# The middle bf16 part of a projection made on GpSimd, and the slots of transposes, expert and post steps placed anew

## The chip, the cores and the metric

The kernel runs on one core of a Trainium2 chip. The metric is the device time of one launch in microseconds. An engine's name in the rows: PE is TensorE, DVE VectorE, ACT ScalarE, POOL GpSimd, SP SyncE.

## The reference

Eight sequences of 512 tokens, 128 features, in fp32. Differential attention with 16 heads of size 8, then a layer norm, then a mixture of 8 experts of which each token uses 2, then a layer norm again. Cut to what is computed:

```python
q, k1, k2, v = (split_heads(x @ W.T) for W in (Wq, Wk1, Wk2, Wv))
a = softmax(causal(q @ k1.T * SCALE)) - sigmoid(lambda_logit) * softmax(causal(q @ k2.T * SCALE))
a = a / maximum(sum(abs(a), -1), 1e-6)
x = layernorm(x + merge_heads(a @ v) @ Wo.T)
xn = layernorm(x) * gamma + beta
w, idx = top_k(softmax(xn @ router_w.T / 1.5), 2)
h = silu(einsum('btd,edf->betf', xn, W1))
y = einsum('betf,efd->betd', h, W2)
out = layernorm(sum over e of wdense[e] * y[e] + x)
```

## The kernel before

**Slots.** All five engines run the same program of bodies; a body has 40 slots (SLOTS), one for each chunk of a batch's attention. A chunk is up to 512 score columns of one head pair: eight pairs times five kinds of chunk, which differ in how many query tiles they hold. Body b does the attention of batch b, prepares batch b+1 (the "prep" steps), and carries the "post" steps of the batches before: slot 48 of a post step means slot 8, one body later. Body -1 is the prologue; bodies 8 to 10 are the tail, in which only post steps are left. Each engine goes through its slots in order; between engines there are only semaphores. So a number in a table of slots sets the place of a step in each engine's queue, and nothing else.

**A chunk's way.** In slot c TensorE makes the scores of chunk c, twice (k = 0 and 1 for the two key sets), and VectorE takes their maxima (neg_max). In slot c+1 (LAG_EXP) ScalarE makes the exponentials into a ring of 7 (EXP_RING). VectorE makes the reciprocals of the sums (inv_l2). In slot c+4 (LAG_DIFF) GpSimd scales the second exponential and subtracts the first (a one-input operation at L623, a two-input one at L627); for one kind in five VectorE does it (L977). In slot c+4 as well (LAG_TRANS) TensorE transposes the difference into the one bank `trans`. In slot c+5 ScalarE copies it out (LAG_COPY), and VectorE sums its absolute values (LAG_ABS). From slot c+6 on TensorE multiplies with the values (LAG_PV). TensorE's transposes come last in a slot, ahead of the next slot's scores:

```python
for n, c in chunks(b, stages, slot, LAG_TRANS):
    pe.wait_ge(*diff_ready(n, c))
    pe.wait_ge(diffT_copied.sem, diffT_copied.after(m, used + 1))
```

**A projection step** ("proj", three of them: q, k1, k2) splits its fp32 result into three bf16 parts. TensorE multiplies in the step's slot, ScalarE makes part 0 (L716) in the same slot. One slot later VectorE makes `rest`, the result less part 0 (L854), and part 1, its cast (L858). Two slots later GpSimd makes part 2, `rest` less part 1 (L634). `rest` is one buffer: VectorE waits for part 2 of the step before. SyncE stores the parts PARTS_SLOT slots after the step, and loads the stack for the next batch's scores from slot STACK_SLOT on.

**Post steps.** "spread", "den_T", "divide" and "out_proj" end the attention: the division (L872) makes attnT on VectorE a slot after its number, TensorE's output projection (L1054) waits for it. "scatter" steps are indirect DMAs that GpSimd issues two slots after their number (L643); each sends 128 rows to their place in the list sorted by expert. "gather" steps bring the results back (L652). "hidden" and "expert" steps are the two matmuls of one of 15 tiles of sorted rows, with ScalarE's tanh between them and VectorE's hT (L933).

Of the kernel before, what the change touches and what calls it, by code (L numbers as in the profile page):

```python
# [52 lines left out]

LAG_EXP = 1
LAG_DIFF = 4
LAG_TRANS = 4
LAG_COPY = LAG_TRANS + 1
LAG_ABS = 5
LAG_DEN = LAG_ABS + 1
# [16 lines left out]


PV_ORDER = (1, 3, 2, 0)
V_SLOT = 7
PV_STEPS = ((7, 0, ((1, 0), (1, 1))), (8, 0, ((3, 0), (3, 1))), (9, 0, ((3, 2), (3, 3), (2, 0))),  # L80
            (9, 1, ((2, 1), (2, 2))), (9, 2, ((0, 0),)))


SIDE = {}
POST_SLOTS = {"spread": 8, "den_T": 10, "divide": 11, "out_proj": 12, "norms": 17, "xn_T": 21, "logits": 23, "router_exp": 24, "count": 29, "place": 31, "sorted": 43, "norm3": 96, "finish": 98}
HIDDEN_SLOTS = (45, 47, 49, 51, 53, 55, 59, 60, 64, 66, 68, 70, 72, 74, 76)
EXPERT_SLOTS = (48, 50, 52, 54, 56, 58, 62, 63, 67, 69, 71, 73, 75, 76, 78)
WEIGHT_SLOTS = (41, 43, 45, 47, 49, 51, 55, 56, 61, 62, 62, 66, 68, 69, 69)
TURN_SLOTS = (44, 51, 58, 66)
Y_OUT_SLOTS = (57, 67, 77, 83)  # L90
SCATTER_SLOTS = (31, 32, 33, 34, 35, 36, 37, 38)
GATHER_SLOTS = (82, 83, 85, 85, 86, 88, 89, 90)
COMBINE_SLOTS = (86, 86, 88, 90, 90, 91, 92, 93)
STACK_SLOT = 31
WEIGHTS_AHEAD = 4
PARTS_SLOT = 4
PREP_SLOTS = (15, 18, 23, 24, 25)


def units_of(c):  # L100
# [74 lines left out]
PARTS_STORED = (3, len(STORED), len(STORED))  # L175
# [19 lines left out]
def build(nc, x, wqT, wk1T, wk2T, wvT, woT, lam, gamma, beta, rwT, w12, out):  # L195
    ctx = ExitStack()
    with ctx:
# [37 lines left out]
        parts = sb("parts", [P, 3, 3, T], BF16)  # L235
        rest = sb("rest", [P, T])
# [79 lines left out]
        rest_made = signal("rest_made", 3)  # L316
        mid_made = signal("mid_made", 3)
        lo_made = signal("lo_made", 3)
        parts_out = signal("parts_out", sum(PARTS_STORED), 16)
# [46 lines left out]
        router_exp = signal("router_exp", 1)  # L366
# [202 lines left out]
        def _(pool):  # L569
# [29 lines left out]
            def body(b, stages):  # L599
                for slot in range(SLOTS):  # L600
                    for n, c in chunks(b, stages, slot, LAG_DIFF):
                        pair, kind = divmod(c, KINDS)
                        ring = ring_e(n, c)
                        count = pair * len(SUM_SETS) + SUM_SET_OF[kind] + 1
# [24 lines left out]
                    for task, n, bank in side_tasks(b, slot, 2 * LAG_SIDE):  # L629
                        name = task[1]  # L630
                        if name == "proj":
                            z = task[2]
                            pool.wait_ge(mid_made.sem, mid_made.after(n, z + 1))
                            nc.gpsimd.tensor_tensor(parts[:, z, 2, :], rest[:, :], parts[:, z, 1, :],  # L634
                                                    ALU.subtract).then_inc(lo_made.sem, 1)
# [128 lines left out]
        def _(dve):  # L764
# [69 lines left out]
            def body(b, stages):  # L834
                for slot in range(SLOTS):
# [10 lines left out]
                    for task, n, bank in side_tasks(b, slot, LAG_SIDE):  # L846
                        name = task[1]
                        if name == "proj":

                            z = task[2]  # L850
                            dve.wait_ge(psum_of(task).sem, psum_of(task).after(n, psum_count[task]))
                            dve.wait_ge(hi_made.sem, hi_made.after(n, z + 1))
                            dve.wait_ge(lo_made.sem, lo_made.after(n, z))
                            nc.vector.scalar_tensor_tensor(out=rest[:, :], in0=bank[:, :],  # L854
                                                           scalar=SCALE if z == 0 else 1.0, in1=parts[:, z, 0, :],
                                                           op0=ALU.mult, op1=ALU.subtract).then_inc(rest_made.sem, 1)
                            dve.wait_ge(rest_made.sem, rest_made.after(n, z + 1))
                            nc.vector.tensor_copy(parts[:, z, 1, :], rest[:, :]).then_inc(mid_made.sem, 1)  # L858
                        if name == "spread":

                            dve.wait_ge(den_done.sem, den_done.after(n, 4))
# [27 lines left out]
                        if name == "logits":  # L889
                            dve.wait_ge(psum_of(task).sem, psum_of(task).after(n, psum_count[task]))  # L890
                            logits = bank[:, 0:NT * E].rearrange("p (t e) -> p t e", t=NT)
# [72 lines left out]
                    for n, c in chunks(b, stages, slot, LAG_EXP + 2):  # L964
                        pair, kind = divmod(c, KINDS)
                        if kind in DVE_KINDS:
# [3 lines left out]
                            count = pair * len(DVE_KINDS) + DVE_KINDS.index(kind) + 1  # L970
# [209 lines left out]
```

## Time and profile before

| what | us |
|---|---|
| device time, median of 3 runs | 1151.64 |
| lowest and highest | 1149.92, 1158.81 |
| the profiled execution | 1164.99 |
| its span | 1163.2 |

The profiled execution took 13.35 us more than the median. Its first 46 us are the prologue, with the constants, the weights and the first projections. Seven batches then follow each other at up to 129 us a batch, and from about 1026 us on only post steps are left. The page gives busy shares; what an engine waits for stands in the view of waits and, in brackets behind an instruction, in the timeline ("[1.59 <-POOL exps L627]": idle for 1.59 us until GpSimd's L627 was done).

### The profile page before, as it was taken

The numbers are of one execution on the slowest core, as the hardware profiler recorded it, in microseconds if no ns is written. First come the engines' busy times: TensorE is split into PE (matmuls) and PEld (weight loads), VectorE is DVE, ScalarE is ACT, GpSimd is POOL, SyncE is SP. The second block draws the span as 40 slices with busy tenths as digits, with TensorE's granted clock in tenths as the row PEclk, the third lists the DMA queues.
The fourth block names the chain that finished last, engine by engine and source line by source line (L and its number), as shares of the span: only waits on it lengthen the run. The fifth ranks groups of instructions, "written<-read, shape, count | busy, mean of one in ns | idle before, by whom it ended". The sixth has DMA issues, their size and how long they took to land.

```text
span 1163.2 us, 27864 instructions
## 1 busy us (share of the span) xinstructions
PE 917.6 (79%) x8522; PEld 730.0 (63%) x8522; DVE 948.4 (82%) x2449; ACT 842.8 (72%) x2706; POOL 838.7 (72%) x1120
## 2 busy tenths in 40 slices
PE   2478867868888888978898979978897888968572
PEld 1255645647677676757676767757675777758561
DVE  1499999879998999979998999889998999725132
ACT  1499978679888788887878878887878878723130
POOL 3388977697768987798768977798769976851503
PEclk9588888679999799988998899988998999878696
DMA  3603400533246524662347415652347322245462
GB/s 102 176 2 95 107 1 16 138 93 124 77 143 167 164 71 128 176 188 72 104 135 181 145 57 154 157 179 92 114 130 193 116 73 83 79 142 189 162 208 62
DMA packets 117045, 139.38 MB, mean 120 GB/s; under 512 B 11042, under 2 KB 99490, under 8 KB 116898
## 3 DMA queue, kind: packets, MB, share of 16 engines
q1 hardware_dynamic: 112802, 129.21, 38.0%
q0 software_dynamic: 4096, 8.40, 2.5%
q8 instruction: 69, 1.13, 0.4%
q14 instruction: 78, 0.64, 0.2%
HBM read 107.81 MB, written 29.75 MB: 118 GB/s over the span
## 4 chain that ended last, share of the span: by engine, by line
DVE 31%; PE 18%; POOL 16%; issue 15%; ACT 12%; DMA 5%; SPq 2%; DVEq 1%; another core or an unknown queue 0%; POOLq 0%; ACTq 0%
DVE neg_max L988 13%; ACT exps L697 7%; DVE abs_sum L998 5%; POOL exps L627 5%; POOL exps L623 5%; POOL x_sorted_dram L643 4%; PE trans L1150 3%; ACT diffT L704 3%; PE side L1093 2%; PE scores L1116 2%; DVE hT L933 2%; DMA w_sb<-w_dram 2%; PE side L1099 2%; PE scores L1093 1%; DVE acc L945 1%
## 5 line engine op out<-in xcount | busy, mean ns | idle before, releaser
L697 ACT ACTIVATE exps<-scores,neg_max 128x512 f32<-128x512 f32 (+3 forms) x1024 | 542.0, 548 | 113.0 <-DVE neg_max L988 106.9
L988 DVE TENSOR_REDUCE neg_max<-scores 128x1 f32<-128x512 f32 (+3 forms) x896 | 423.5, 524 | 58.0 <-PE scores L1118 53.5
L627 POOL TENSOR_TENSOR exps<-exps 128x512 f32<-128x512 f32 x256 | 326.1, 1274 | 21.4
L623 POOL TENSOR_SCALAR exps<-exps,inv_l,lam_l 128x384 f32<-128x384 f32 (+3 forms) x448 | 273.6, 618 | 91.5 <-DVE inv_l L963 79.2
L1150 PE MATMUL trans<-ident,exps 128*128 128x128 f32 x1280 | 236.4, 314 | 117.6 <-ACT diffT L704 61.9
L1116 PE MATMUL scores<-stack 72*128 72x512 bf16 (+3 forms) x1024 | 275.3, 337 | 16.3 <-DMA stack<-parts_dram 15.8
L1150 PEld LDWEIGHTS trans<-ident,exps 128*128 128x128 f32 x1280 | 158.9, 158 | 179.6 <-issue 99.3
L697 ACT ACTIVATION_READ_ACCUMULATOR exps<-scores,neg_max 128x1 f32 x1024 | 232.6, 227 | 0.0
L704 ACT ACTIVATE diffT<-trans 128x512 f32<-128x512 f32 x320 | 195.7, 612 | 45.7 <-PE trans L1150 44.4
L998 DVE TENSOR_REDUCE abs_sum<-exps 128x1 f32<-128x512 f32 (+3 forms) x448 | 222.6, 519 | 5.6 <-POOL exps L627 5.6
L1118 PE MATMUL scores<-causal_bf,ident_bf 128*128 128x128 bf16 x1024 | 211.0, 239 | 0.0
L1116 PEld LDWEIGHTS scores<-stack 72*128 72x128 bf16 x1024 | 111.5, 109 | 69.1 <-DMA stack<-parts_dram 16.0
L1093 PE MATMUL side<-xgT,w_sb 128*128 128x128 f32 x792 | 123.9, 305 | 3.6 <-DMA w_sb<-w_dram 1.7
L1099 PE MATMUL side<-w_sb,hT 128*128 128x128 f32 x824 | 116.4, 285 | 6.8 <-DVE hT L933 5.6
L1093 PEld LDWEIGHTS side<-xgT,w_sb 128*128 128x128 f32 x792 | 109.3, 213 | 11.2 <-issue 3.3
L1118 PEld LDWEIGHTS scores<-causal_bf,ident_bf 128*128 128x128 bf16 x1024 | 111.8, 109 | 7.0
L1099 PEld LDWEIGHTS side<-w_sb,hT 128*128 128x128 f32 x824 | 103.4, 197 | 14.3 <-DVE hT L933 5.8
L1139 PE MATMUL heads<-diffT,v_sb 128*32 128x128 f32 x2560 | 108.1, 287 | 2.8 <-issue 2.8
L652 POOL DMA_INDIRECT y_back<-y_sorted_dram,place_int x64 | 65.6, 1026 | 47.1 <-issue 45.7
L643 POOL DMA_INDIRECT x_sorted_dram<-xh,place_int x64 | 68.4, 1069 | 40.5 <-DVE owner_int L924 30.6
L1139 PEld LDWEIGHTS heads<-diffT,v_sb 128*32 128x32 f32 x2560 | 62.8, 112 | 37.7 <-issue 22.5
L750 ACT ACTIVATE tanh_sb<-side 128x512 f32<-128x512 f32 x99 | 60.3, 609 | 32.3 <-PE side L1093 29.6
(138 smaller groups left out, 916.5 us busy)
## 6 DMA issues: line engine op xcount, KB each, us to landing
w_sb<-w_dram SPq DMA_DIRECT2D x120, 512.0 KB
stack<-parts_dram SPq DMA_DIRECT2D x288, 96.0 KB
parts_dram<-parts SPq DMA_DIRECT2D x104, 128.0 KB, 2.4
xg<-x_sorted_dram SPq DMA_DIRECT2D x24, 256.0 KB
y_sorted_dram<-y_sorted SPq DMA_DIRECT2D x24, 256.0 KB, 4.3
x_in<-x_dram SPq DMA_DIRECT2D x8, 256.0 KB, 4.4
x_res<-x_dram SPq DMA_DIRECT2D x8, 256.0 KB, 4.6
o_dram<-y_out SPq DMA_DIRECT2D x8, 256.0 KB, 2.3
```

Of the source, the lines that this page charges most:

```text
L623: nc.gpsimd.tensor_scalar(diff[:, ring, col:col + w], exps[:, ring, 1, col:col + w], inv_l2[:, i:i + 1], lam_l1[:, i:i + 1], ALU.mult, ALU ...
L627: nc.gpsimd.tensor_tensor(diff[:, ring, :], diff[:, ring, :], exps[:, ring, 0, :], ALU.subtract)\
L697: nc.scalar.activation(exps[:, ring, k, col:col + w], scores[:, c % 2, k, col:col + w], ACT.Exp, bias=neg_max[:, c % 2, k, i:i + 1], accum ...
L704: nc.scalar.activation(diffT[:, ring_d(n, c), :], trans[:, :], ACT.Copy)\
L988: nc.vector.tensor_reduce(neg_max[:, c % 2, k, i:i + many], scores[:, c % 2, k, col:col + many * w].rearrange("p (i w) -> p i w", w=w), AX ...
L998: nc.vector.tensor_reduce(abs_sum[:, place:place + (many - 1) * step + 1:step], diff[:, ring_e(n, c), col:col + many * w].rearrange("p (i ...
L1093: last = nc.tensor.matmul(bank[:, f * P:(f + 1) * P], w12_sb[:, w, f * P:(f + 1) * P], xgT[:, j // NT % 2, j % NT, :], start=True, stop=True)
L1099: last = nc.tensor.matmul(bank[:, 0:D], hT[:, (n * TILES + j) % 2, f, :], w12_sb[:, (n * TILES + j) % WEIGHTS_AHEAD, F + f * D:F + (f + 1) ...
L1116: nc.tensor.matmul(scores[:, c % 2, k, col:col + w], stack[:, 0, h, t * P:(t + 1) * P], stack[:, 1 + k, h, 0:w], start=True, stop=False)
L1118: last = nc.tensor.matmul(scores[:, c % 2, k, col + w - P:col + w], ident_bf[:, :], causal_bf[:, :], start=False, stop=True)
L1139: last = nc.tensor.matmul(heads[k * STRIP:(k + 1) * STRIP, t * P:(t + 1) * P], v_sb[:, i, NG * k + g, :], diffT[:, ring_d(n, source), col: ...
L1150: last = nc.tensor.transpose(trans[:, i * P:(i + 1) * P], diff[:, ring_e(n, c), i * P:(i + 1) * P], ident[:, :])
```

## The change

Three things.

1. The cast that makes part 1 of a projection goes from VectorE to GpSimd, directly ahead of GpSimd's subtraction. GpSimd now waits for `rest`, and for the stores of the batch before, as ScalarE does.
2. LAG_TRANS goes from 4 to 5. LAG_COPY and LAG_PV hang on it and go to 6 and 7. LAG_DIFF and LAG_ABS stay at 4 and 5.
3. The slots of many steps are new. The second and third projection go from slots 23 and 24 to 22 and 23, the division from 11 to 10, five of the scatter steps up by a slot, stores and stack loads down by 3 and 2, and the late expert steps down by one.

```diff
-LAG_TRANS = 4
+LAG_TRANS = 5
 LAG_COPY = LAG_TRANS + 1
...
-V_SLOT = 7
+V_SLOT = 8
...
-HIDDEN_SLOTS = (45, 47, 49, 51, 53, 55, 59, 60, 64, 66, 68, 70, 72, 74, 76)
+HIDDEN_SLOTS = (45, 46, 49, 51, 53, 55, 59, 60, 64, 66, 68, 70, 73, 75, 77)
...
-SCATTER_SLOTS = (31, 32, 33, 34, 35, 36, 37, 38)
+SCATTER_SLOTS = (31, 32, 32, 34, 34, 35, 36, 37)
...
-STACK_SLOT = 31
+STACK_SLOT = 33
 WEIGHTS_AHEAD = 4
-PARTS_SLOT = 4
-PREP_SLOTS = (15, 18, 23, 24, 25)
+PARTS_SLOT = 7
+PREP_SLOTS = (15, 18, 22, 23, 24)
...
                         if name == "proj":
                             z = task[2]
+                            pool.wait_ge(rest_made.sem, rest_made.after(n, z + 1))
+                            pool.wait_ge(parts_out.sem, parts_out.after(n - 1, sum(PARTS_STORED)))
+                            nc.gpsimd.tensor_copy(parts[:, z, 1, :], rest[:, :]).then_inc(mid_made.sem, 1)
                             pool.wait_ge(mid_made.sem, mid_made.after(n, z + 1))
                             nc.gpsimd.tensor_tensor(parts[:, z, 2, :], rest[:, :], parts[:, z, 1, :],
                                                     ALU.subtract).then_inc(lo_made.sem, 1)
...
                                                            scalar=SCALE if z == 0 else 1.0, in1=parts[:, z, 0, :],
                                                            op0=ALU.mult, op1=ALU.subtract).then_inc(rest_made.sem, 1)
-                            dve.wait_ge(rest_made.sem, rest_made.after(n, z + 1))
-                            nc.vector.tensor_copy(parts[:, z, 1, :], rest[:, :]).then_inc(mid_made.sem, 1)
```

GpSimd, before, around the second and third projection step of a batch; exps, inv_l and lam_l belong to the differences, parts and rest to the projection:

```order
L614 TENSOR_TENSOR lam_l<-sums,lam_all 128x3 [waits exp_done]
L623 TENSOR_SCALAR exps<-exps,inv_l,lam_l 128x384 [waits inv_l2_done,lam_l1_done]
L623 TENSOR_SCALAR exps<-exps,inv_l,lam_l 128x128
L627 TENSOR_TENSOR exps<-exps 128x512 [waits scaled_done]
L634 TENSOR_TENSOR parts<-rest,parts 128x512 [waits mid_made]
L614 TENSOR_TENSOR lam_l<-sums,lam_all 128x2 [waits exp_done]
L623 TENSOR_SCALAR exps<-exps,inv_l,lam_l 128x256 [waits inv_l2_done,lam_l1_done]
L623 TENSOR_SCALAR exps<-exps,inv_l,lam_l 128x256
L627 TENSOR_TENSOR exps<-exps 128x512 [waits scaled_done]
L634 TENSOR_TENSOR parts<-rest,parts 128x512 [waits mid_made]
```

And after:

```order
L614 TENSOR_TENSOR lam_l<-sums,lam_all 128x3 [waits exp_done]
L635 CAST parts<-rest 128x512 [waits parts_out,rest_made]
L637 TENSOR_TENSOR parts<-rest,parts 128x512 [waits mid_made]
L623 TENSOR_SCALAR exps<-exps,inv_l,lam_l 128x384 [waits inv_l2_done,lam_l1_done]
L623 TENSOR_SCALAR exps<-exps,inv_l,lam_l 128x128
L627 TENSOR_TENSOR exps<-exps 128x512 [waits scaled_done]
L635 CAST parts<-rest 128x512 [waits parts_out,rest_made]
L637 TENSOR_TENSOR parts<-rest,parts 128x512 [waits mid_made]
L614 TENSOR_TENSOR lam_l<-sums,lam_all 128x2 [waits exp_done]
```

The second step now stands ahead of the difference that it stood behind, directly behind a three-column product, and each step has a cast of its own.

GpSimd, before, at the first four scatter steps of a batch (the DMA rows):

```order
L643 DMA x_sorted_dram<-xh,place_int 1920x128 [waits placed,xh_done,sorted_in,sorted_cleared]
L614 TENSOR_TENSOR lam_l<-sums,lam_all 128x3 [waits exp_done]
L643 DMA x_sorted_dram<-xh,place_int 1920x128
L623 TENSOR_SCALAR exps<-exps,inv_l,lam_l 128x384 [waits inv_l2_done,lam_l1_done]
L623 TENSOR_SCALAR exps<-exps,inv_l,lam_l 128x128
L627 TENSOR_TENSOR exps<-exps 128x512 [waits scaled_done]
L643 DMA x_sorted_dram<-xh,place_int 1920x128
L614 TENSOR_TENSOR lam_l<-sums,lam_all 128x2 [waits exp_done]
L623 TENSOR_SCALAR exps<-exps,inv_l,lam_l 128x256 [waits inv_l2_done,lam_l1_done]
L623 TENSOR_SCALAR exps<-exps,inv_l,lam_l 128x256
L627 TENSOR_TENSOR exps<-exps 128x512 [waits scaled_done]
```

And after:

```order
L646 DMA x_sorted_dram<-xh,place_int 1920x128 [waits placed,xh_done,sorted_in,sorted_cleared]
L614 TENSOR_TENSOR lam_l<-sums,lam_all 128x3 [waits exp_done]
L646 DMA x_sorted_dram<-xh,place_int 1920x128 x2
L623 TENSOR_SCALAR exps<-exps,inv_l,lam_l 128x384 [waits inv_l2_done,lam_l1_done]
L623 TENSOR_SCALAR exps<-exps,inv_l,lam_l 128x128
L627 TENSOR_TENSOR exps<-exps 128x512 [waits scaled_done]
L614 TENSOR_TENSOR lam_l<-sums,lam_all 128x2 [waits exp_done]
L623 TENSOR_SCALAR exps<-exps,inv_l,lam_l 128x256 [waits inv_l2_done,lam_l1_done]
L623 TENSOR_SCALAR exps<-exps,inv_l,lam_l 128x256
L627 TENSOR_TENSOR exps<-exps 128x512 [waits scaled_done]
L646 DMA x_sorted_dram<-xh,place_int 1920x128 x2
```

The third scatter step moved ahead of the difference behind the second, and the fifth stands beside the fourth.

TensorE, before, at the start of the first batch's attention, from the second half of slot 4's score matmuls on; trans are the transposes:

```order
L1116 MATMUL scores<-stack 128x384
L1118 MATMUL scores<-causal_bf,ident_bf 128x128
L1116 MATMUL scores<-stack 128x128
L1118 MATMUL scores<-causal_bf,ident_bf 128x128
L1150 MATMUL trans<-ident,exps 128x128 x4
L1116 MATMUL scores<-stack 128x512
L1118 MATMUL scores<-causal_bf,ident_bf 128x128
L1116 MATMUL scores<-stack 128x512
L1118 MATMUL scores<-causal_bf,ident_bf 128x128
L1150 MATMUL trans<-ident,exps 128x128 x4
```

And after, at the same place:

```order
L1117 MATMUL scores<-stack 128x384
L1119 MATMUL scores<-causal_bf,ident_bf 128x128
L1117 MATMUL scores<-stack 128x128
L1119 MATMUL scores<-causal_bf,ident_bf 128x128
L1117 MATMUL scores<-stack 128x512
L1119 MATMUL scores<-causal_bf,ident_bf 128x128
L1117 MATMUL scores<-stack 128x512
L1119 MATMUL scores<-causal_bf,ident_bf 128x128
L1151 MATMUL trans<-ident,exps 128x128 x4
L1117 MATMUL scores<-stack 128x384
L1119 MATMUL scores<-causal_bf,ident_bf 128x128
L1117 MATMUL scores<-stack 128x128
```

The first chunk's transposes stand one chunk of scores later, and so do all that follow.

## Rows read from the trace of the kernel before

**Rows 1.** The page, busy us, share of the span, instructions of each engine.
```profile
PE 917.6 (79%) x8522; PEld 730.0 (63%) x8522; DVE 948.4 (82%) x2449; ACT 842.8 (72%) x2706; POOL 838.7 (72%) x1120
```

**Rows 2.** The page, shares of the chain that ended last, by engine.
```profile
DVE 31%; PE 18%; POOL 16%; issue 15%; ACT 12%; DMA 5%; SPq 2%; DVEq 1%; another core or an unknown queue 0%; POOLq 0%; ACTq 0%
```

**Rows 3.** Windows: busy us (x instructions) of PE, PEld, DVE, ACT, POOL; clock, DMA.
```profile
core 0: us, PE busy (x) PEld busy (x) DVE busy (x) ACT busy (x) POOL busy (x), PEclk, DMA share, GB/s
560.00:688.00 128.00, 110.66 (x1061) 89.69 (x1059) 117.65 (x304) 103.40 (x335) 103.39 (x136) 0.89 0.46 134
650.00:660.00 10.00, 8.02 (x87) 6.59 (x88) 9.79 (x24) 7.65 (x27) 9.06 (x11) 0.99 0.22 67
```

**Rows 4.** Timeline of DVE, projections of one batch: start us, us, engine, line.
```profile
581.34 0.69 DVE L854 SCALAR_TENSOR_TENSOR rest<-side,parts 128x512 f32<-128x512 f32 x1 [0.56 <-ACT parts L716]
582.07 0.43 DVE L858 CAST parts<-rest 128x512 bf16<-128x512 f32 x1
...
585.27 0.68 DVE L854 SCALAR_TENSOR_TENSOR rest<-side,parts 128x512 f32<-128x512 f32 x1
585.99 0.76 DVE L858 CAST parts<-rest 128x512 bf16<-128x512 f32 x1
```

**Rows 5.** Groups by form: busy us, mean ns | idle before, releaser.
```profile
L623 POOL TENSOR_SCALAR exps<-exps,inv_l,lam_l 128x512 f32<-128x512 f32 x64 | 49.3, 771 | 46.2 <-DVE inv_l L963 43.4
...
L634 POOL TENSOR_TENSOR parts<-rest,parts 128x512 bf16<-128x512 f32 x24 | 27.8, 1158 | 42.6 <-DVE parts L858 42.6
...
L858 DVE CAST parts<-rest 128x512 bf16<-128x512 f32 x24 | 13.8, 574 | 0.8
...
L597 POOL CAST ident_bf<-ident 128x128 bf16<-128x128 f32 x1 | 0.3, 291 | 0.1
```

**Rows 6.** Waits from 225 to 945 us: us in total, times, longest us.
```profile
PE trans L1150 <- POOL exps L627: 44.7, 25, 2.9
...
DVE neg_max L988 <- PE scores L1118: 32.4, 28, 2.9
...
POOL parts L634 <- DVE parts L858: 18.8, 15, 2.4
```

**Rows 7.** Timeline of PE, two late transposes.
```profile
633.94 1.12 PE L1150 MATMUL trans<-ident,exps 128*128 128x128 f32 x4 [1.59 <-POOL exps L627]
...
637.95 1.12 PE L1150 MATMUL trans<-ident,exps 128*128 128x128 f32 x4 [1.61 <-POOL exps L627]
```

**Rows 8.** Timeline of DVE: late maxima (L988), absolute sums (L998) behind them.
```profile
251.33 1.42 DVE L988 TENSOR_REDUCE neg_max<-scores 128x1 f32<-128x384 f32 x4 [2.95 <-PE scores L1118]
...
635.80 1.42 DVE L988 TENSOR_REDUCE neg_max<-scores 128x1 f32<-128x384 f32 x4 [1.04 <-PE scores L1118]
637.14 0.73 DVE L998 TENSOR_REDUCE abs_sum<-exps 128x1 f32<-128x384 f32 x2
639.82 1.29 DVE L988 TENSOR_REDUCE neg_max<-scores 128x2 f32<-128x512 f32 x2 [1.94 <-PE scores L1118]
641.02 0.68 DVE L998 TENSOR_REDUCE abs_sum<-exps 128x2 f32<-128x512 f32 x1
...
896.32 1.29 DVE L988 TENSOR_REDUCE neg_max<-scores 128x2 f32<-128x512 f32 x2 [2.70 <-PE scores L1118]
```

**Rows 9.** Timeline of POOL, scatter stretch of the same batch.
```profile
612.24 1.00 POOL L643 DMA_INDIRECT x_sorted_dram<-xh,place_int  x1 [0.17 <-issue]
614.22 1.52 POOL L623 TENSOR_SCALAR exps<-exps,inv_l,lam_l 128x384 f32<-128x384 f32 x2 [0.97 <-DVE inv_l L963]
...
632.63 1.26 POOL L627 TENSOR_TENSOR exps<-exps 128x512 f32<-128x512 f32 x1
...
636.63 1.27 POOL L627 TENSOR_TENSOR exps<-exps 128x512 f32<-128x512 f32 x1
```

**Rows 10.** Timeline of PE, tail, output projection of the last batch.
```profile
1047.36 1.13 PE L1054 MATMUL scores<-wo_sb,attnT 128*128 128x128 f32 x8 [1.21 <-DVE attnT L872]
```

**Rows 11.** Line L977: ns min/median/max, first and last start.
```profile
L977 DVE SCALAR_TENSOR_TENSOR exps<-exps,coef x64: 750/963/1210, 48.9 to 1012.2; 128x512 f32<-128x512 f32 x64
```

More of the change, by code:

```diff
@@ L84 @@
 SIDE = {}
-POST_SLOTS = {"spread": 8, "den_T": 10, "divide": 11, "out_proj": 12, "norms": 17, "xn_T": 21, "logits": 23, "router_exp": 24, "count": 29, "place": 31, "sorted": 43, "norm3": 96, "finish": 98}
-HIDDEN_SLOTS = (45, 47, 49, 51, 53, 55, 59, 60, 64, 66, 68, 70, 72, 74, 76)
-EXPERT_SLOTS = (48, 50, 52, 54, 56, 58, 62, 63, 67, 69, 71, 73, 75, 76, 78)
-WEIGHT_SLOTS = (41, 43, 45, 47, 49, 51, 55, 56, 61, 62, 62, 66, 68, 69, 69)
-TURN_SLOTS = (44, 51, 58, 66)
+POST_SLOTS = {"spread": 7, "den_T": 10, "divide": 10, "out_proj": 12, "norms": 17, "xn_T": 21, "logits": 23, "router_exp": 24, "count": 29, "place": 31, "sorted": 43, "norm3": 96, "finish": 98}
+HIDDEN_SLOTS = (45, 46, 49, 51, 53, 55, 59, 60, 64, 66, 68, 70, 73, 75, 77)
+EXPERT_SLOTS = (48, 50, 52, 54, 56, 58, 62, 63, 67, 69, 71, 73, 76, 77, 79)
+WEIGHT_SLOTS = (41, 43, 45, 47, 49, 51, 55, 56, 61, 62, 62, 66, 69, 70, 70)
+TURN_SLOTS = (44, 51, 58, 65)
 Y_OUT_SLOTS = (57, 67, 77, 83)
-SCATTER_SLOTS = (31, 32, 33, 34, 35, 36, 37, 38)
-GATHER_SLOTS = (82, 83, 85, 85, 86, 88, 89, 90)
-COMBINE_SLOTS = (86, 86, 88, 90, 90, 91, 92, 93)
-STACK_SLOT = 31
+SCATTER_SLOTS = (31, 32, 32, 34, 34, 35, 36, 37)
+GATHER_SLOTS = (82, 83, 85, 85, 87, 88, 88, 90)
+COMBINE_SLOTS = (86, 86, 88, 90, 91, 91, 91, 93)
+STACK_SLOT = 33
 WEIGHTS_AHEAD = 4
-PARTS_SLOT = 4
-PREP_SLOTS = (15, 18, 23, 24, 25)
+PARTS_SLOT = 7
+PREP_SLOTS = (15, 18, 22, 23, 24)
 def units_of(c):
```

## The prediction

> **What bounds the kernel now.** I read the page's busy shares first: VectorE leads with 948.4 of 1163.2 us and GpSimd has 838.7 [rows 1]. An average hides stages, so the chain of waits comes next: VectorE carries 31% of it and GpSimd 16% [rows 2]. The windows, cut to one batch (128 us), settle it: VectorE works 117.65 of the 128 us, TensorE 110.66, GpSimd 103.39, and the other full batches read alike [rows 3]. VectorE bounds the attention loop. A microsecond taken from it there, busy or idle, is a microsecond off the batch, if the others can follow. Last I read where VectorE idles. Between 225 and 945 us (six batches less their ends) its largest idle term is 32.4 us of waiting for the score matmuls; TensorE in its turn waits 44.7 us, before transposes, for GpSimd's differences [rows 6]. The timelines tie the two together: the transposes at 633.94 and 637.95 us start 1.59 and 1.61 us late for GpSimd [rows 7], and the maxima at 635.80 and 639.82 us start 1.04 and 1.94 us late for the scores that are queued behind those transposes [rows 8].
>
> **The change part by part.**
>
> The cast leaves VectorE. It ran 24 times in 13.8 us; the three of the prologue took some 0.43 us each, so 12.5 us lie in the loop [rows 5]. Nothing covers them: at 585.27 us the subtraction and then the cast (0.76 us) run without a gap [rows 4]. Term one: -12.5 us. It holds only where VectorE is the late engine, which rows 3 say of all but the tail.
>
> The cast comes to GpSimd, 24 times. No row shows a 128x512 cast there. Bounds: the 128x128 cast took 0.29 us, the 128x512 one-input operation 0.77, the 128x512 two-input one that writes bf16 1.16 [rows 5]. I take 0.65, near the one-input row, since the cast has one input; the ends 0.3 and 1.16 stay for the range. Three a batch make 2 us beside 104 busy. The cover is GpSimd's own waiting at this step: 18.8 us in 15 times, 1.25 us each, all for VectorE's cast [rows 6]. GpSimd now waits for the subtraction alone, so it starts at least 0.43 us sooner and ends 0.65 - 0.43 = 0.2 us later. The first step of a batch stays in its slot; the second and third move one slot forward, so that GpSimd meets the second where it has only a three-element product to make. Loop: 0. Prologue, where the three projections run one after the other: 3 x 0.2 = +0.6 us.
>
> A rule against this: the Trainium skill (GPSIMD Engine Reference, section 4, engine selection) sends elementwise work to VectorE, with GpSimd about twice as slow on two-input operations. The rows agree on slower (0.77 us against VectorE's usual 0.43 for one input). By that rule alone the sum would lose the 12.5 us and pay for a longer step. I don't follow it, since VectorE is the full engine here and GpSimd is not.
>
> The transposes go one chunk later (LAG_TRANS 4 to 5, and with it the copies and the value products). GpSimd makes the difference of a chunk in that chunk's slot plus four. TensorE, in order, asked for it in the same slot and held the next scores back; now it asks 3.2 us (a slot, 128 over 40) later. Every wait for GpSimd in rows 7 is shorter than that. Of VectorE's idle time, 14 waits in those six batches stand right behind such transposes, from the first at 251.33 (2.95 us) to the last at 896.32 (2.70 us) [rows 8]; they sum to 23.2 us, 3 to 5.7 a batch, and rows 8 show a pair. What is late next? VectorE's own sum of |difference|, in slot plus five as before. GpSimd ended those two chunks at 633.90 and 637.90 (start plus 1.27) [rows 9]; VectorE took them up at 637.14 and 641.02 [rows 8]. Slack 3.2 and 3.1 us, and VectorE will come 3 us sooner: it just fits. TensorE's later transposes meet GpSimd again at that distance, and in the gather slots GpSimd stays full (9.06 of 10 us, [rows 3]). So I book three quarters: term two, -17 us, with 0 and -23 as its ends. The rings (seven chunks of exponentials, twelve of transposed differences) aren't nearer to blocking: an exponential that reuses a slot comes eight slots after its chunk, three slots behind the new transpose.
>
> Scatter steps move up. The third now stands beside the second, ahead of a product for which GpSimd waited 0.97 us at 614.22 [rows 9]. A step of 1.07 us with its 0.15 us of issue fills that hole; the product starts 0.3 us later, and all behind it 0.9 us sooner. While GpSimd is full this is what keeps term two alive; alone it counts once, where the last batch's attention ends on GpSimd: -1 us.
>
> The division goes from slot 11 to 10, ahead of an expert step on VectorE. Inside the loop the projection's wait for it stops TensorE, not VectorE. In the tail it is on the path: 1.21 us at 1047.36 [rows 10]. Term: -1 us.
>
> The rest: expert, weight, turn, gather and combine steps move by a slot, and in the tail they keep their order among themselves, so 0. Stores of the parts and loads of the stack go some two slots later on SyncE; the first stack load still has seven slots (22 us) ahead of the next batch, and no wait for the stack shows in the loop, so 0 too.
>
> Sum: -12.5 - 17 - 1 - 1 + 0.6 = -30.9 us. The profiled execution took 1164.99 us, 13 more than the median 1151.64. The terms are stalls and casts of every execution, so I take them off the median whole: 1121, rounded to **1122 us**, or -2.6%.
>
> **The rivals.**
>
> (A) As above: 1108 to 1135.
>
> (B) The stall only changes place. GpSimd is full from the first scatter to the last gather; if the 3.1 us of slack in rows 8 and 9 are used up, VectorE waits at its absolute sums in place of the maxima. For it: the slack fits to a tenth of a microsecond. Against it: the 0.9 us that the scatter steps give back. Then only the casts count: 1152 - 12 = 1140, and 1136 to 1146 around it.
>
> (C) GpSimd's casts slow VectorE down. VectorE's product of exponentials, with two SBUF inputs, takes between 750 and 1210 ns [rows 11], and its casts between 0.43 and 0.76 us [rows 4]. So operations of equal size stretch, as if they stood in line for something. If each of 21 casts costs a VectorE operation that 0.46 us, 9.7 us of term one are gone: 1132 with term two, 1149 without. The Trainium skill (GPSIMD Engine Reference, key points) says that GpSimd shares its SBUF interfaces with VectorE, and that two-port modes and two SBUF inputs contend. By it the cast that leaves was a victim itself, so I count this as partial.
>
> (D) Slower. VectorE may not overwrite rest before GpSimd has subtracted from it; in a batch two of the three subtractions wait for that. Between those at 581.34 and 585.27 lie 3.93 us [rows 4]; 0.69 for the subtraction itself, 0.65 and 1.16 for GpSimd's two steps leave 1.4 us. If GpSimd comes to the cast with a chunk's difference still ahead of it (1.52 + 1.27 us at the most in [rows 9]), VectorE stands 1.4 us, at the head of a slot, with the maxima queued behind it and ScalarE waiting for those; with two chunks ahead, 4.2. Twice a batch, seven batches: 20 to 59 us. Above 2.2 us each it outweighs all gains; at 3 us it gives 1163. Against it: GpSimd waited for VectorE there in all 15 cases [rows 6].
>
> (E) The lag does nothing since TensorE is held by the copies of ScalarE anyway, and the casts are covered by something that I don't see: 1147 to 1155.
>
> **How the numbers follow.** A 0.60, B 0.20, C alone 0.06, D 0.08, E 0.06. The executions before spread over 1149.92 to 1158.81, so within 1% is what a measurement here can't tell from nothing; that line lies at 1140. All of A, half of B and a third of C are faster by more: 0.72. Half of B, the rest of C, E and a little of D: 0.20. The rest of D: 0.08. The range's low end takes term two whole, term one with the shortened waits around it, and some five microseconds of the other waits for scores (32.4 less 23.2): 1107. The high end lets in most of B: 1143.
>
> **What the profile would show.** Term one: no cast on VectorE, 24 on GpSimd near 0.65 us, VectorE's busy time down by 12 to 14 us. Term two: TensorE's wait for GpSimd before transposes from 44.7 to under 15 us, VectorE's for scores from 32.4 to under 15, and batches of 123 to 125 us in place of 128.6. B: waits of VectorE's absolute sums for GpSimd of over 10 us. C: the product of exponentials above its median of 963 ns [rows 11]. D: waits of the subtraction for GpSimd inside the loop. The prediction fails if TensorE, at 110.66 us of 128 with its transposes unblocked, becomes late by itself, or if GpSimd's cast is far over a microsecond.

## The result, and the profile after

The changed kernel takes 1138.13 us in the median of 6 runs (1134.45 to 1139.79), the one before 1155.38 in the median of 6 (1149.92 to 1158.81). The ratio is 0.9858, 95% interval 0.9837 to 0.9880: 1.4% faster, or 16.4 us. The forecast was 1122 us, 2.6% or 30.9 us. The time lies in its range, by the room that the range leaves for rival B, and the gain is half of what was booked.

The two profiled executions differ by more, in span 1163.2 against 1137.3 us. VectorE's place_of, once a batch, marks the batches: in the profile after, the first and the seventh of these stand at

```profile
226.89 0.22 DVE L906 TENSOR_TENSOR place_of<-hit,side 128x64 f32<-128x64 f32 x1 [3.55 <-PE side L1080]
...
978.46 0.22 DVE L906 TENSOR_TENSOR place_of<-hit,side 128x64 f32<-128x64 f32 x1 [0.99 <-PE side L1080]
```

and in the profile before at

```profile
230.17 0.22 DVE L905 TENSOR_TENSOR place_of<-hit,side 128x64 f32<-128x64 f32 x1 [3.54 <-PE side L1079]
...
991.88 0.22 DVE L905 TENSOR_TENSOR place_of<-hit,side 128x64 f32<-128x64 f32 x1 [2.19 <-PE side L1079]
```

So a batch took 126.9 us before and 125.3 after: 10 us in the six together. The stretch behind, to the eighth mark, makes another 10 of the difference, and it varied between 71 and 84 us from one profiled execution to the next, with and without the change, so I don't count it as a gain. The forecast's 128.6 us belong to the full batches, the second to the fifth between these marks: they took 128.7 us each before and take 127.4 after, not the 123 to 125 of the forecast.

The page after, busy time, beside [rows 1]:

```profile
PE 908.5 (80%) x8522; PEld 726.7 (64%) x8522; DVE 935.6 (82%) x2425; ACT 841.1 (74%) x2706; POOL 846.0 (74%) x1144
```

VectorE is 12.8 us less busy, as forecast, in a kernel that gained 16. The batch of [rows 3], after:

```profile
560.00:688.00 128.00, 108.02 (x1082) 87.09 (x1082) 120.46 (x309) 105.70 (x343) 105.73 (x141) 0.95 0.45 134
```

VectorE still leads. Between the first and the seventh mark VectorE's time divides so (one profiled execution each; the last row is the run with the later turn, below):

| kernel | us | VectorE busy | VectorE idle |
|---|---|---|---|
| before | 761.7 | 701.2 | 60.6 |
| changed | 751.6 | 693.6 | 58.0 |
| changed, later turn | 735.3 | 695.6 | 39.7 |

So of these 10 us some 7.6 are work that left VectorE, and 2.6 came from its idle time, where term two had 15 for six of the seven batches. From single executions this split is good to a few us, no better. The groups of the projection, beside [rows 5]:

```profile
L637 POOL TENSOR_TENSOR parts<-rest,parts 128x512 bf16<-128x512 f32 x24 | 29.9, 1244 | 1.9
...
L635 POOL CAST parts<-rest 128x512 bf16<-128x512 f32 x24 | 15.1, 629 | 27.7 <-issue 16.3 <-DVE rest L857 11.2
```

The cast on GpSimd is 0.63 us, against 0.65 assumed. The waits from 225 to 945 us, beside [rows 6]:

```profile
PE trans L1151 <- ACT diffT L707: 35.6, 41, 2.4
...
DVE neg_max L989 <- PE scores L1119: 28.7, 27, 4.4
...
PE trans L1151 <- POOL exps L627: 13.1, 15, 2.6
...
PE side L1086 <- DMA xg<-x_sorted_dram: 11.7, 5, 4.1
...
POOL parts L635 <- DVE rest L857: 8.0, 5, 1.8
...
DVE abs_sum L999 <- POOL exps L627: 1.3, 4, 0.4
```

This view holds the main reading. TensorE's wait for GpSimd fell from 44.7 to 13.1 us, as the forecast had it (under 15). VectorE's wait for scores ought to have gone with it, and it hardly moved: 32.4 to 28.7. The new line is L1086, the first turn step of a batch, in which TensorE transposes the sorted rows (xg): 0.6 us before, 11.7 now. Before, in the same view:

```profile
PE side L1085 <- DMA xg<-x_sorted_dram: 0.6, 2, 0.4
```

TensorE's waits for ScalarE's copies grew as well, from 23.7 to 35.6 us; the run with lag and turn below has 36.5 of them beside a short wait of VectorE, so they are not what holds VectorE. One place with the turn late, TensorE first:

```profile
758.86 0.63 PE L1151 MATMUL trans<-ident,exps 128*128 128x128 f32 x4 [0.45 <-ACT diffT L707]
...
759.97 0.22 PE L1119 MATMUL scores<-causal_bf,ident_bf 128*128 128x128 bf16 x1
763.62 1.09 PE L1086 MATMUL side<-ident,xg 128*128 128x128 f32 x4 [3.44 <-DMA xg<-x_sorted_dram]
764.64 1.08 PE L1140 MATMUL heads<-diffT,v_sb 128*32 128x128 f32 x16
765.65 1.12 PE L1151 MATMUL trans<-ident,exps 128*128 128x128 f32 x4
766.56 0.64 PE L1117 MATMUL scores<-stack 72*128 72x512 bf16 x1
```

VectorE, at the same time:

```profile
763.44 0.19 DVE L846 SCALAR_TENSOR_TENSOR guard<-sums,abs_sum 128x32 f32<-128x32 f32 x1
767.41 1.29 DVE L989 TENSOR_REDUCE neg_max<-scores 128x1 f32<-128x512 f32 x2 [3.78 <-PE scores L1119]
```

SyncE's queue ahead of it:

```profile
748.81 3.67 SPq L535 DMA_DIRECT2D stack<-parts_dram  x9
...
755.16 0.37 SPq L516 DMA_DIRECT2D y_sorted_dram<-y_sorted  x1
755.63 3.99 SPq L498 DMA_DIRECT2D xg<-x_sorted_dram  x4
```

and the last scatter, on GpSimd:

```profile
749.42 0.98 POOL L646 DMA_INDIRECT x_sorted_dram<-xh,place_int  x1 [0.17 <-issue]
```

Read from the end: VectorE's maxima wait 3.78 us for scores; these stand in TensorE's queue behind the turn, which waits 3.44 us for the loads of xg; SyncE issues the loads at 755.63, behind the last scatter (it ended at 750.40) and behind nine loads of the stack and four other transfers. In five of the six batches the maxima behind this step waited for scores, 4.42, 3.22, 1.95, 3.78 and 2.50 us, 15.9 of the 28.7. The wait that the later transposes took from the middle of the queue stands at the turn, four slots into the batch.

### The profile page after: what moved, and what is told of

Its sections match the earlier page's. It is cut to its first block and busy times, and to the rows that moved or that the text cites. A ratio compares the mean times of both kernels' runs of the same rounds, so it can differ in the third digit from the quotient of the medians.

```text
span 1137.3 us, 27887 instructions
## 1 busy us (share of the span) xinstructions
PE 908.5 (80%) x8522; PEld 726.7 (64%) x8522; DVE 935.6 (82%) x2425; ACT 841.1 (74%) x2706; POOL 846.0 (74%) x1144
## 5 line engine op out<-in xcount | busy, mean ns | idle before, releaser
L1117 PE MATMUL scores<-stack 72*128 72x512 bf16 (+3 forms) x1024 | 272.6, 335 | 16.6 <-DMA stack<-parts_dram 15.6
L700 ACT ACTIVATION_READ_ACCUMULATOR exps<-scores,neg_max 128x1 f32 x1024 | 235.8, 230 | 0.0
L1094 PE MATMUL side<-xgT,w_sb 128*128 128x128 f32 x792 | 121.3, 301 | 1.9 <-DMA w_sb<-w_dram 1.0
L646 POOL DMA_INDIRECT x_sorted_dram<-xh,place_int x64 | 66.8, 1043 | 44.7 <-DVE owner_int L925 29.9
L753 ACT ACTIVATE tanh_sb<-side 128x512 f32<-128x512 f32 x99 | 60.6, 613 | 25.8 <-PE side L1094 25.1
```

The costliest lines, as they stand in the source:

```text
L700: nc.scalar.activation(exps[:, ring, k, col:col + w], scores[:, c % 2, k, col:col + w], ACT.Exp, bias=neg_max[:, c % 2, k, i:i + 1], accum ...
L1094: last = nc.tensor.matmul(bank[:, f * P:(f + 1) * P], w12_sb[:, w, f * P:(f + 1) * P], xgT[:, j // NT % 2, j % NT, :], start=True, stop=True)
L1117: nc.tensor.matmul(scores[:, c % 2, k, col:col + w], stack[:, 0, h, t * P:(t + 1) * P], stack[:, 1 + k, h, 0:w], start=True, stop=False)
```

## Experiments

Every kernel was timed against the kernel before on one chip. Chips differed by up to 1.2%, so ratios to the kernel before are compared, with their 95% intervals. Waits are from 225 to 945 us of the profiled execution. Theory W: the gain of the later transposes comes back as the turn's wait.

**The cast alone.** The kernel before, with the cast on GpSimd ahead of its subtraction, with the waits of the change.

```diff
-                            nc.vector.tensor_copy(parts[:, z, 1, :], rest[:, :]).then_inc(mid_made.sem, 1)
...
+                            nc.gpsimd.tensor_copy(parts[:, z, 1, :], rest[:, :]).then_inc(mid_made.sem, 1)
```

> The kernel before with one edit: the cast of each projection on GpSimd; all slots and lags as before. Theory W (the casts made the gain, and what the later transposes freed came back as another wait): 11 to 13 us faster than before, ratio near 0.990, as term one had it. Rival G (the casts only trade VectorE time for waits on GpSimd, the gain is in the slots): within 4 us of before, and VectorE's subtraction waits for GpSimd in the loop.

Measured: 0.9964 (0.9941 to 0.9988), 4 us. W's 11 to 13 us did not come. The number is nearer to rival G's, but the wait of VectorE's subtraction for GpSimd that G names shows nowhere in the view. The time that leaves VectorE is worth a third of itself here. The two main waits stay near those of [rows 6]:

```profile
PE trans L1151 <- POOL exps L627: 44.1, 23, 2.8
...
DVE neg_max L989 <- PE scores L1119: 33.6, 33, 2.9
```

**The later transposes alone.**

```diff
-LAG_TRANS = 4
+LAG_TRANS = 5
-V_SLOT = 7
+V_SLOT = 8
```

> The kernel before with two numbers changed: LAG_TRANS 4 to 5 and V_SLOT 7 to 8. Theory W: 1 to 5 us faster, ratio 0.996 to 0.999; TensorE's wait for GpSimd before transposes halves, and waits of TensorE's turn step for the sorted rows appear, with VectorE's maxima late behind them. My prediction's term two: 17 us faster, ratio 0.985. A third view, that GpSimd's rate sets the stretch from scatter to gather: no change, and VectorE waits at its absolute sums.

Measured: 0.9990 (0.9968 to 1.0012), nothing. Yet the wait that they aim at is gone:

```profile
DVE neg_max L988 <- PE scores L1118: 29.7, 24, 4.5
...
PE trans L1150 <- POOL exps L627: 17.1, 14, 2.2
...
PE side L1085 <- DMA xg<-x_sorted_dram: 12.1, 5, 3.3
```

27.6 us off the wait for GpSimd, 11.5 us on the turn's, 2.7 off VectorE's. W holds in the kernel before as well; the forecast's 0.985 does not.

**The changed kernel with the cast back on VectorE.**

```diff
-                            nc.gpsimd.tensor_copy(parts[:, z, 1, :], rest[:, :]).then_inc(mid_made.sem, 1)
...
+                            nc.vector.tensor_copy(parts[:, z, 1, :], rest[:, :]).then_inc(mid_made.sem, 1)
```

> The changed kernel with the cast back on VectorE, every new slot and lag kept. Theory W: 11 to 13 us slower than the changed kernel, so 3 to 5 us faster than before, ratio near 0.996. Rival G: within 4 us of the changed kernel, ratio near 0.987.

Measured: 0.9905 (0.9877 to 0.9933), between the two expectations. The cast is worth 0.5% in the changed kernel, 5 us; two thirds of the gain are elsewhere.

**The changed kernel with the turn a slot later.**

```diff
-TURN_SLOTS = (44, 51, 58, 65)
-HIDDEN_SLOTS = (45, 46, 49, ...
+TURN_SLOTS = (45, 51, 58, 65)
+HIDDEN_SLOTS = (46, 47, 49, ...
```

> The changed kernel with the first turn step a slot later (44 to 45) and the first two hidden steps with it (45, 46 to 46, 47). Theory W: the maxima that stood 1.95 to 4.42 us behind the turn's wait in five batches (15.9 us in all) start in time, and the kernel is 7 to 14 us faster than the changed one, ratio 0.974 to 0.980 to before. Rival S (GpSimd's rate sets the stretch): the wait moves on to VectorE's absolute sums or to the next transposes, and the time stays within 3 us of the changed kernel, ratio near 0.986.

Measured: 1122.85 us, 0.9735 (0.9705 to 0.9764), faster than both kernels and just past W's range. Its full batches took 123.8 us, as forecast. Its waits:

```profile
PE trans L1151 <- ACT diffT L707: 28.5, 32, 2.5
PE trans L1151 <- POOL exps L627: 27.6, 27, 2.6
...
DVE neg_max L989 <- PE scores L1119: 12.3, 19, 1.1
```

The line of the turn is gone from the view, and VectorE waits 12.3 us for scores in place of 28.7. TensorE waits twice as long for GpSimd as in the changed kernel (27.6 against 13.1 us), and the kernel is faster all the same: I read from it that only the waits that reach VectorE count. In its timeline the turn starts 8.4 us behind the issue of its loads (744.03) and finds them there:

```profile
752.47 0.60 PE L1086 MATMUL side<-ident,xg 128*128 128x128 f32 x4
...
753.58 0.66 PE L1151 MATMUL trans<-ident,exps 128*128 128x128 f32 x4
```

**The lag back, in the changed kernel.** LAG_TRANS 4 and V_SLOT 7.

> The changed kernel with LAG_TRANS back at 4 and V_SLOT at 7; cast on GpSimd and new slots stay. Theory W (what the later transposes give is taken back at TensorE's turn step): near the changed kernel, 1136 to 1142, the waits for GpSimd before transposes back above 35 us in six batches, the turn's wait for the sorted rows down from 11.7 to under 6. Rival P (the later transposes are worth most of the forecast 17 us by themselves and something else ate it): 1148 to 1155.

Measured: 1.0012 (0.9985 to 1.0040). Here W's number fell and the ratio is the one of rival P (1148 to 1155 us; measured 1156.99): in the changed kernel the lag is worth 1.5%. P's reason is not borne out, since the lag by itself gave 0.1%. The turn's wait did not fall without it either:

```profile
DVE neg_max L989 <- PE scores L1119: 47.4, 47, 4.6
PE trans L1151 <- POOL exps L627: 36.7, 30, 3.3
...
PE side L1086 <- DMA xg<-x_sorted_dram: 15.6, 6, 3.7
```

So something in the new slots raises the turn's wait by itself, and the lag takes part of that back. The scatter run below shows what.

**The later turn alone**, on the kernel before.

```diff
-TURN_SLOTS = (44, 51, 58, 66)
-HIDDEN_SLOTS = (45, 47, 49, ...
+TURN_SLOTS = (45, 51, 58, 66)
+HIDDEN_SLOTS = (46, 47, 49, ...
```

> The kernel before with the first turn step in slot 45 in place of 44 and the first hidden step in 46 in place of 45; nothing else. In the kernel before the turn waits for the sorted rows only 0.6 us in six batches, against 11.7 in the changed one. Theory W: nothing to win here, 1150 to 1156, within 0.3% of the kernel before; the later turn pays only together with the change. Rival Q (a later turn is worth its 15 us in any kernel, by the place of its matmuls and not by its wait): 1137 to 1143.

Measured: 0.9993 (0.9977 to 1.0009), 1152.05 us. W's number; the rival is out.

**Later turn, with the cast back on VectorE.**

> The kernel with the later turn (1122.85 us) with the cast back on VectorE. Theory W in full: with the turn's wait gone VectorE is the engine that sets the batch, and the cast costs what it did by its time, 21 x 0.55 = 12 us: 1132 to 1137. Rival R (the cast is worth little whatever the turn does, since the stretch of scatter steps goes by GpSimd, and since other operations of VectorE stretch when it leaves): 4 us, 1125 to 1129.

Measured: 1134.57 us, 0.9821 (0.9754 to 0.9888). The cast is worth 0.86%, 10 us: W's number. The four executions spread over 19 us, though, and the interval holds rival R's range (1125 to 1129 us, ratios of 0.976 to 0.979) too: the rival is not out.

**Later turn, with the lag back.**

> The kernel with the later turn (1122.85 us) with LAG_TRANS back at 4 and V_SLOT at 7. Theory W: the later transposes are worth most of the forecast 17 us once the turn no longer waits: 1134 to 1141, and TensorE's waits for GpSimd before transposes rise from 27.6 to above 40 us. Rival S (the lag is worth next to nothing anywhere and the gain of the later turn is its own): 1121 to 1127.

Measured: 0.9922 (0.9893 to 0.9951). The lag is worth 1.9% here. In us this is 1142.52, 1.5 above W's range and 15 above the rival's; TensorE's wait for GpSimd is 48.0 us, as W has it.

**Lag and later turn, on the kernel before.** The two diffs above together.

> The kernel before with the later transposes (LAG_TRANS 5, V_SLOT 8) and the first turn step in slot 45 (first hidden step in 46); the cast stays on VectorE and all other slots are the old ones. Each of the two alone moved the time by 0.1%. Theory W (the stall that the later transposes take away came back at the turn, so the two pay only together): 1133 to 1140, no wait of the turn for its rows, VectorE's waits for scores in six batches under 20 us. Rival S (the gain needs the new scatter and stack slots too): 1144 to 1151.

Measured: 0.9821 (0.9773 to 0.9870), 21 us. This is the test of W: two edits that are worth 0.1% each alone give 1.8% together, and the rival's 1144 to 1151 would be a ratio of 0.992 at the least. (The bounds in us were written for a chip on which the kernel before took 1153; here it took 1167.) The waits:

```profile
PE trans L1150 <- POOL exps L627: 18.8, 19, 2.7
...
DVE neg_max L988 <- PE scores L1118: 16.0, 25, 2.2
```

**Cast, lag and later turn, on the kernel before.**

> As the run with lag and turn, with the cast on GpSimd too; it differs from the fastest kernel so far (1122.85 us) only in the slots of scatter, projection, division, stores, stack and late expert steps. Theory W: 6 to 12 us under the run with lag and turn alone, and within 4 us of the fastest: 1121 to 1129. Rival S (the new scatter slots are what makes room on GpSimd): 1133 to 1145.

Measured: 0.9752 (0.9712 to 0.9792). As W has it. With the turn out of the way, all other new slots together are worth 0.2%, less than the interval.

**The stack loads back.** The changed kernel with STACK_SLOT 31 in place of 33.

> The changed kernel with STACK_SLOT back from 33 to 31. SyncE issues the loads of the sorted rows behind nine loads of the stack; with lag 4 and the new slots these came 6 us after the last scatter in place of 3.3 to 3.9. Theory K (the later stack loads hold the sorted rows up in the changed kernel as well): the turn's wait falls from 11.7 us to under 8, the loads are issued within 4 us of the last scatter, 1132 to 1136. Rival (TensorE simply comes too soon and the scatter's landing sets the loads): the turn's wait stays above 10 us, 1136 to 1140.

Measured: 0.9853 (0.9814 to 0.9892), turn's wait 10.8 us. Theory K falls. The last nine loads stand in the body's last slot whatever STACK_SLOT says, and wait there for TensorE's last scores of the batch:

```python
if b + 1 < B and slot == SLOTS - 1:
    stack_part(b + 1, NG - 1)
```

**The new scatter slots alone**, on the kernel before.

```diff
-SCATTER_SLOTS = (31, 32, 33, 34, 35, 36, 37, 38)
+SCATTER_SLOTS = (31, 32, 32, 34, 34, 35, 36, 37)
```

> The kernel before with the new SCATTER_SLOTS alone. Forecast term: 1 us off, 1149 to 1154, nothing that a run can tell from no change. Rival T (scatter steps a slot earlier let GpSimd through its full stretch sooner and bring the sorted rows sooner): 1143 to 1148, the waits for GpSimd before transposes under 38 us in six batches.

Measured: 1.0039 (1.0004 to 1.0073), slightly slower, which neither expectation had. Its waits:

```profile
DVE neg_max L988 <- PE scores L1118: 47.3, 40, 4.0
PE trans L1150 <- POOL exps L627: 41.9, 28, 3.0
...
PE side L1085 <- DMA xg<-x_sorted_dram: 10.4, 6, 2.9
```

SyncE's timeline shows the second thing that holds the loads of xg:

```profile
636.56 3.66 SPq L535 DMA_DIRECT2D stack<-parts_dram  x9
640.26 0.41 SPq L543 DMA_DIRECT2D x_in<-x_dram  x1
...
642.90 0.37 SPq L516 DMA_DIRECT2D y_sorted_dram<-y_sorted  x1
643.37 3.74 SPq L498 DMA_DIRECT2D xg<-x_sorted_dram  x4
```

The last scatter ended at 637.70. The loads left 5.7 us behind it, 0.1 behind the store ahead of them in the queue: they were held not by the scatter but by the queue, whose nine stack loads begin when TensorE has made the batch's last scores. A sooner scatter is no use as long as TensorE comes late to those. Here, from the second batch on, the nine loads start 1.1 to 1.2 us ahead of the last scatter's end; with lag 5 and the same scatter slots (the next run) 3.4 to 3.5 us ahead, so that the scatter counts.

**Lag and scatter slots, on the kernel before.**

> The kernel before with the later transposes (LAG_TRANS 5, V_SLOT 8) and the new SCATTER_SLOTS, nothing else. Times are given as ratios to the kernel before, since chips differ by over 1%. Alone they measured 0.999 and 1.0039. Theory X (the sooner last scatter gives the later transposes a part of the slack that they lack at the turn): 0.988 to 0.993, as the changed kernel with its cast back has it (0.9905). Rival Y (the other new slots do that): 0.997 to 1.005.

Measured: 0.9958 (0.9929 to 0.9988), between the two expectations. The turn's wait is half of that with the lag alone: 6.0 against 12.1. The scatter slots give 0.3% behind the lag, no more than the error of that difference, and cost 0.4% without it.

**Cast and lag, on the kernel before.**

> The kernel before with the cast on GpSimd and the later transposes, all slots old. Theory X: the two add up to little, 0.994 to 0.998 of the kernel before, with the turn's wait above 10 us in six batches. Rival (cast and lag without the slots are the changed kernel already): 0.984 to 0.988.

Measured: 0.9927 (0.9897 to 0.9957), just under theory X's 0.994, with 13.3 us at the turn. The cast is worth 0.6% behind the lag.

**The changed kernel with the old scatter slots.**

> The changed kernel (0.9858 of the kernel before) with the old SCATTER_SLOTS. Theory X: it loses what the sooner scatter gives, 0.993 to 0.998, and the turn's wait stays at 11 us or rises. Rival Y: 0.984 to 0.988, no change.

Measured: 0.9918 (0.9887 to 0.9950), just under theory X's range; rival Y is out. The turn's wait is 12.4 us. The scatter slots are worth 0.6% in the changed kernel. Without them VectorE meets GpSimd at its absolute sums:

```profile
DVE abs_sum L999 <- POOL exps L627: 9.4, 7, 1.6
```

against 1.3 us with them.

**The turn two slots later.** The changed kernel with TURN_SLOTS from 46 and HIDDEN_SLOTS from (47, 47, ...).

> The changed kernel with the first turn step in slot 46 and both of its hidden steps in 47. In slot 45 it has no wait left in the six batches (0.9735 of the kernel before). Theory W (only the wait was worth anything): no further gain, 0.972 to 0.978. Rival Q (the place of the turn's matmuls matters by itself): 0.965 to 0.970, or above 0.98 if two hidden steps in one slot bunch up.

Measured: 0.9784 (0.9741 to 0.9828). No gain over slot 45 (0.9735), and a hair above W's range. The wait was the price, not the place.

Side by side, each edit's worth by what else was in the kernel (difference of two ratios; from their intervals each is good to 0.2 to 0.5%, the two casts behind the later turn to 0.6 and 0.7%):

| edit | on what | worth |
|---|---|---|
| later transposes | nothing else | 0.1% |
| | cast | 0.4% |
| | scatter slots | 0.8% |
| | cast and all new slots | 1.5% |
| | later turn | 1.7% |
| | cast, new slots, later turn | 1.9% |
| cast | nothing else | 0.4% |
| | lag | 0.6% |
| | lag and new slots | 0.5% |
| | lag and later turn | 0.7% |
| | lag, new slots, later turn | 0.9% |
| later turn | nothing else | 0.1% |
| | lag | 1.7% |
| | cast and lag | 1.8% |
| | cast and all new slots | 0.9% |
| | cast, lag and all new slots | 1.2% |
| scatter slots | nothing else | -0.4% |
| | lag | 0.3% |
| | cast, lag and the other slots | 0.6% |

## Why the prediction was half right

**Term two, the later transposes (17 us), is the step that failed,** together with the 0 that the prediction books for the turn among "the rest". The first half of the mechanism was right: the wait of TensorE for GpSimd went from 44.7 to 13.1 us, as forecast. What failed is the question "what is late next?". I answered it for VectorE's absolute sums alone, where the slack of 3.1 us indeed just fitted (1.3 us of waits), and never asked it of TensorE's own next wait. That was the turn, which had hardly any slack before either. In the trace before:

```profile
516.91 0.63 PE L1085 MATMUL side<-ident,xg 128*128 128x128 f32 x4 [0.38 <-DMA xg<-x_sorted_dram]
```

Those 0.38 us, with 0.19 in the first of the six batches, say that TensorE arrived as the data did; in the other four it came 6.1 to 7.1 us after the first load's start, where with the lag alone, waiting, it had the rows after 5.9 to 6.4. That leaves about a microsecond. A TensorE freed by 3 us must wait there for what the loads don't gain. Lag alone 0.1%, turn alone 0.1%, both 1.8%: that part is shown. With the turn moved, the term measures 1.7 to 1.9%, 20 to 22 us, so the 17 were not even too many; by itself the lag gets none of them. In the changed kernel itself, taking the lag back costs 1.5%, but into a state that the new slots had made worse (15.6 us at the turn).

The turn's price in the changed kernel is the step from 0.9858 to 0.9735: 1.2%, 14 us, and the forecast had 14.5 us too much. With the turn a slot later the kernel is 2.65% faster than before, where 2.6% was forecast. That the sums agree so well is in part luck, since the parts don't: the lag then measures 20 to 22 us and the cast 8 to 10.

The 23.2 us in 14 waits from which I took the term are slightly too many: counted again, 13 maxima stand behind transposes that waited for GpSimd, 22.0 us in all. The term would hardly change.

**Term one, the cast (12.5 us), was too large.** The work left VectorE as forecast: 12.8 us less busy, no cast on it, 24 on GpSimd at 0.63 us. It is worth 0.4 to 0.9%, 4 to 10 us, and 5 in the changed kernel. It grows as waits go: the condition that I wrote, "only where VectorE is the late engine", I then took as fulfilled all through the loop from shares of busy time [rows 3]. My explanation is that in the stretches in which TensorE waits for GpSimd or for the sorted rows VectorE waits with it, and time saved ahead of them turns into waiting. Which stretches ate how much of the 12.5 was not measured; that they do is argued from the trend of the table, whose rows for the cast differ by no more than their errors.

**The scatter slots (1 us)** were thought of as relief for GpSimd. They do keep the absolute sums free, as written (9.4 us of waits without them, 1.3 with them), and behind the lag they are worth 0.3 to 0.6%. Alone they cost 0.4% (0.04 to 0.73%) and TensorE stands 10.4 us at the turn, while the loads are held by SyncE's queue; that this wait makes the loss is read from the views, not tried.

**The small terms.** The wait ahead of the last output projection (1.21 us in [rows 10]) is gone; the division was not tried alone. The three casts of the prologue were to cost 0.6 us; the first place_of comes 3.3 us sooner, and which edit did that wasn't tried.

**The rivals.** (B) had the right shape, a stall that only changes place, and the wrong place. (C): GpSimd's casts were to raise VectorE's product above its median of 963 ns. It reads, after,

```profile
L978 DVE SCALAR_TENSOR_TENSOR exps<-exps,coef x64: 750/958/1817, 48.9 to 995.9; 128x512 f32<-128x512 f32 x64
```

The median did not move. The longest went from 1.21 to 1.82 us, but it is 1.77 us with the lag alone and 1.76 with the scatter slots alone, where all casts are on VectorE, so it isn't the cast that does it. And VectorE's busy time fell by 12.8 us where the casts had taken 13.8: other operations took back 1 us at the most, not 9.7. The shared interfaces of the Trainium skill (GPSIMD Engine Reference, key points) may stand behind the spread; no run here separates them. The rule of the same page of the Trainium skill that sends elementwise work to VectorE (section 4, engine selection) would have lost by 0.4 to 0.9% here. Its factor of two is for two inputs; one input it calls roughly line-rate, and the trace agrees: 629 ns a cast on GpSimd, 574 on VectorE. (D) did not occur: inside the loop no wait of the subtraction for GpSimd shows in the view from 225 to 945 us. (E) is out: lag and turn as a pair give 1.8%, and the cast alone 0.4%, beyond its interval.

Open: why lag and all new slots (0.9905) stand 0.5% below lag and scatter slots alone (0.9958). The intervals just touch, and the projection slots, which may be the reason, were not tried by themselves. Nor is it shown why the turn's wait is longest, 15.6 us, with all new slots and the old lag.

## What to carry to other kernels

When a stall is taken out of an engine that works in order, follow that engine, not only its consumers, to its next wait, and look there for small waits now: a few tenths of a microsecond mean no slack, and no wait at all need not mean that there is any. Then move the step that waits in the same edit; two edits worth nothing alone can be worth 2% as a pair, and trying them one at a time would have thrown both away. A step that waits for a DMA may be held by the DMA queue's order rather than by the data's maker.

## What the runs showed that I had not expected

The stall at the turn also comes with a longer stretch at TensorE's lower clock. In the changed kernel the transposes take 0.63 us at 758.86 and 1.12 at 765.65, behind 3.44 us of waiting, and the granted clock from 764 to 769 us is 0.59, near the lower of the two levels:

```profile
764.00:769.00 5.00, 5.00 (x40) 3.52 (x42) 1.59 (x3) 3.19 (x10) 4.51 (x7) 0.59 0.58 207
```

With the turn a slot later the same place in the batch reads 0.93, and its transposes 0.66 us:

```profile
751.00:756.00 5.00, 5.00 (x64) 3.87 (x60) 4.97 (x14) 4.92 (x17) 4.67 (x6) 0.93 0.80 303
```

It is not that the clock falls only there: in all three kernels it is also low for some microseconds ahead of the turn. Without the stall it is back when the turn starts, with the stall only later. In the 5 us from the start of the turn the granted clock of the six batches was 1.00, 1.00, 1.00, 0.94, 1.00 and 0.99 before, 0.65, 0.62, 0.50, 0.68, 0.55 and 0.50 in the changed kernel, and 1.00, 0.91, 1.00, 1.00, 1.00 and 0.98 with the later turn. The first of the changed kernel's six had no wait at the turn itself, so the stall is not the whole reason; and over the six batches together the clock hardly differs (0.91, 0.91, 0.92). What it cost in time was not measured.

The loads of xg took longer where other transfers stood just ahead of them in SyncE's queue. Straight behind the nine stack loads and their followers, the four took 3.99 us to issue (755.63 in the changed kernel), and TensorE had them 8.0 us after the start; with a pause ahead, in the run with the lag alone, 2.02 us and 6.1 (no run shows why):

```profile
764.30 2.02 SPq L498 DMA_DIRECT2D xg<-x_sorted_dram  x4
```

```profile
770.40 1.08 PE L1085 MATMUL side<-ident,xg 128*128 128x128 f32 x4 [2.28 <-DMA xg<-x_sorted_dram]
```
